# Block 0's gate and output projection taken out of the last stage and into the last round of the recurrence

## The reference, cut to what matters

```python
o = rwkv7_op(r, w, k2, v, -kk, kk * a)              # the recurrence over time, 2 sequences of 1024
o = o * gn_scale + gn_offset
o = o + rwkv                                        # the "bonus" term
x = x + (o * g) @ W_o                               # gate, then output projection, then residual
# then layer norm of x, a two-way switch, and expert 0 (gelu) or expert 1 (relu) per token
```

## Time and profile before

| what | us |
|---|---|
| median of 3 runs (1360.82, 1362.17, 1364.11) | 1362.17 |
| the profiled execution's own time | 1361.62 |
| its span, first to last instruction | 1359.6 |
| TensorE busy | 1229.7 (90%) |
| VectorE busy | 862.5 (63%) |
| ScalarE busy | 571.0 (42%) |
| GpSimd busy | 248.2 (18%) |
| last two hops of the recurrence begin | 1196.5 |
| last stage's first instruction | 1201.43 |
| last instruction's end (span) | 1359.6 |

### The profile page before, as it was taken

One profiled execution on the slowest core, in us unless ns is written; L12 is line 12 of the kernel. 1 busy time (PEld: TensorE's weight loads), 2 busy tenths in 40 slices (PEclk: granted clock), 3 DMA queues, 4 the chain that ended last, 5 costly groups with the idle time before them and its releaser, 6 DMA issues. The chain is left out here.

```text
span 1359.6 us, 32622 instructions
## 1 busy us (share of the span) xinstructions
PE 1229.7 (90%) x13048; PEld 714.2 (53%) x13080; DVE 862.5 (63%) x1742; ACT 571.0 (42%) x854; POOL 248.2 (18%) x444
## 2 busy tenths in 40 slices
PE   5769999999999999878999968995999999969998
PEld 2433333333333333254677644442888888857775
DVE  6367878888888888345433364897576666643432
ACT  2314777777777776823133214652211111112221
POOL 4220010000001001040277500233222111000000
PEclk9867999999999999998999988997999999979999
DMA  4310112211111220051143320000200000000000
GB/s 127 54 23 4 29 28 40 41 28 27 28 27 29 40 39 3 3 160 62 32 162 101 119 79 0 0 0 5 76 4 4 4 4 3 4 2 0 16 16 31
DMA packets 33836, 49.47 MB, mean 36 GB/s; under 512 B 11995, under 2 KB 22331, under 8 KB 32955
## 3 DMA queue, kind: packets, MB, share of 16 engines
q1 hardware_dynamic: 29211, 36.55, 12.1%
q0 software_dynamic: 3744, 10.23, 2.4%
q10 hardware_dynamic: 768, 1.05, 0.2%
HBM read 23.63 MB, written 9.31 MB: 24 GB/s over the span
## 5 line engine op out<-in xcount | busy, mean ns | idle before, releaser
L664 DVE TENSOR_REDUCE at_block_max<-at_p_ring 128x4 f32<-128x512 f32 x576 | 367.7, 686 | 76.3 <-PE at_p_ring L570 42.2
L641 ACT ACTIVATE at_probs<-at_p_score,abias 128x1024 f32<-128x1024 f32 (+2 forms) x320 | 318.8, 1029 | 123.2 <-PE at_p_score L600 69.0
L570 PE MATMUL at_p_ring<-kt,qt 64*128 64x128 bf16 (+3 forms) x1152 | 187.2, 284 | 18.5 <-PEq L727 7.4
L615 PE MATMUL at_p_out<-at_probs,at_vs 128*32 128x512 f32 (+3 forms) x1536 | 164.5, 500 | 0.4 <-ACT at_probs L641 0.4
L594 PE MATMUL at_p_score<-qt,kt 64*128 64x512 bf16 (+3 forms) x768 | 146.2, 332 | 5.7 <-ACT at_probs L641 4.8
L570 PEld LDWEIGHTS at_p_ring<-kt,qt 64*128 64x128 bf16 x1152 | 69.9, 95 | 130.4 <-DVE at_block_max L664 86.6
L707 POOL TENSOR_TENSOR at_shift<-shift,at_row_max 128x16 f32<-128x16 f32 x32 | 7.1, 221 | 423.2 <-DVE at_row_max L670 423.2
L594 PEld LDWEIGHTS at_p_score<-qt,kt 64*128 64x128 bf16 x768 | 38.4, 94 | 85.7 <-ACT at_probs L641 55.2
L2055 ACT COPY rc_ta<-rc_bank 128x256 f32<-128x256 f32 x32 | 10.3, 375 | 148.9 <-PE rc_bank L1826 148.9
L2184 PE MATMUL fi_p_in<-fi_xt,w_in 128*128 128x512 f32 x128 | 64.2, 626 | 0.7 <-ACT fi_xt L2221 0.7
L600 PE MATMUL at_p_score<-anticausal,ident 128*128 128x128 bf16 (+1 forms) x384 | 62.3, 244 | 0.0
(11 more groups left out here) (334 smaller groups left out, 2153.9 us busy)
## 6 DMA issues: line engine op xcount, KB each, us to landing
qt<-qparts SPq DMA_DIRECT2D x96, 64.0 KB, 2.4
kt<-kparts SPq DMA_DIRECT2D x96, 64.0 KB, 2.5
rows<-moe_chosen SPq DMA_DIRECT2D x4, 1024.0 KB, 4.8
w_routed<-in_w_routed_dram SPq DMA_DIRECT2D x1, 2816.0 KB
x<-in_x_dram SPq DMA_DIRECT2D x4, 512.0 KB, 8.4
moe_table<-rows SPq DMA_DIRECT2D x4, 512.0 KB, 2.7
out_dram<-x SPq DMA_DIRECT2D x4, 512.0 KB, 2.9
w_down<-in_w_down_dram SPq DMA_DIRECT2D x1, 1408.0 KB
```

What stands on the lines that cost most here:

```text
L570: mm = pe.matmul(bank[:, col:col + nb * P], qt[nxt][h * ROWS:(h + 1) * ROWS, pair, t * P:(t + 1) * P], kt[nxt][h * ROWS:(h + 1) * ROWS, pa ...
L615: mm = pe.matmul(p_out[32 * h:32 * h + 32, left(k):QC], vs[(now - e[2]) % BUFS][:, key, h, :], probs[g % PROBS][:, h % 2, at:at + w], star ...
L641: act.activation(probs[g % PROBS][:, :, 0:len(pairs) * w], p_score[g % 2][:, :, 0:len(pairs) * w], ACT.Exp, bias=abias[:, c * TPB + key:c ...
L664: dve.tensor_reduce(dst, src, AX.X, ALU.max).then_inc(s["fill_used"], 1)
```

## The change

GpSimd computes block 0's gate behind its last `y1`. TensorE computes block 0's projection at the end of the recurrence's last pass, behind the last hop, into banks 2 and 3 of `bank[0]`. VectorE adds it to x as the last thing in the recurrence's block. In the last stage gate(0) and project(0) are gone, add_projection(0) keeps only the statistics, and gate(1) stands behind normalise(0). The tile `gated0` is allocated outside both phases, and the recurrence phase also gets `vec`, `w_out` and `x`.

```diff
+        first_tiles = TB // P                       # 4
@@ TensorE, recurrence
+                def project_first(t, b):
+                    if last(t) and b == 0:
+                        pe.wait_ge(first_gated, EH)
+                        pe.wait_ge(loaded, len(pairs) * 16)
+                        pe.wait_ge(act_did[0], t * ACT_MARKS["each"])
+                        for tile in range(first_tiles):
+                            for h in range(EH):
+                                mm = pe.matmul(bank[0][:, 2 + tile // 2, tile % 2 * E:(tile % 2 + 1) * E],
+                                               gated[:, h, tile * P:(tile + 1) * P], w[:, h, :],
+                                               start=h == 0 and tile % 2 == 0, stop=h == EH - 1, skip_group_check=True)
+                        mm.then_inc(first_out, 1)
+
+                stages.append(project_first)
+                rounds(stages, (ys0, hop0, ys1, hop1, project_first))(pe)
@@ VectorE, recurrence, behind the last advance
+                dve.wait_ge(first_out, 1)
+                dve.tensor_tensor(x[:, 0:first_tiles, :], bank[0][:, 2:4, :].rearrange("p b (t e) -> p (b t) e", e=E),
+                                  x[:, 0:first_tiles, :], ALU.add)
@@ GpSimd, recurrence, behind the last y1
+                pool.wait_ge(y_out[0], first_tiles)
+                for h in range(EH):
+                    pool.tensor_scalar(gated[:, h, :], yt[:, h, 0, :], vec[:, h, VEC["gn_scale"]:VEC["gn_scale"] + 1], None,
+                                       ALU.mult).then_inc(first_scaled, 1)
+                pool.wait_ge(first_scaled, EH)
+                pool.tensor_tensor(gated[:, :, :], gated[:, :, :], data["bonus"][:, :, 0, :], ALU.add).then_inc(first_scaled, 1)
+                pool.wait_ge(first_scaled, EH + 1)
+                for h in range(EH):
+                    pool.tensor_scalar(gated[:, h, :], gated[:, h, :], vec[:, h, VEC["gn_offset"]:VEC["gn_offset"] + 1], None,
+                                       ALU.add).then_inc(first_scaled, 1)
+                pool.wait_ge(first_scaled, 2 * EH + 1)
+                for h in range(EH):
+                    pool.tensor_tensor(gated[:, h, :], gated[:, h, :], data["gt"][:, h, 0, :], ALU.mult).then_inc(first_gated, 1)
@@ last stage
-        gated = [sb(f"gated{i}", [P, EH, TB]) for i in range(2)]
+        gated = [gated0, sb("gated1", [P, EH, TB])]
@@ TensorE
                 def project(n):
-                    pe.wait_ge(gated_ready, (n + 1) * EH)
-                    if n:
-                        pe.wait_ge(tok_read, n)
+                    pe.wait_ge(gated_ready, n * EH)
+                    pe.wait_ge(tok_read, n)
...
-                project(0)
                 turn(0)
@@ VectorE
                 def add_projection(n):
-                    dve.wait_ge(proj_ready, n + 1)
...
-                    c.link(dve.tensor_tensor(tiles, p_work[:, :, :].rearrange("p b (t e) -> p (b t) e", e=E), tiles, ALU.add))
+                    if n:
+                        dve.wait_ge(proj_ready, n)
+                        c.link(dve.tensor_tensor(tiles, p_work[:, :, :].rearrange("p b (t e) -> p (b t) e", e=E), tiles, ALU.add))
...
-                gate(0)
-                gate(1)
                 add_projection(0)
                 normalise(0)
+                gate(1)
```

More of the change, by code:

```diff
@@ L1705, with recurrence_phase @@
 HOP_DONE = marks_of("s0a", "s0", "s1a", "s1")
-def recurrence_phase(nc, data, ident, masks, level_masks, level1_t, eye, yt, loaded, pairs):
+def recurrence_phase(nc, data, ident, masks, level_masks, level1_t, eye, yt, loaded, pairs, vec, w, x, gated):
     with ExitStack() as ctx:
@@ L1728, in recurrence_phase @@
         hop_made, hop_done, y_out = sem("hop_made"), sem("hop_done"), sem("y_out")
+        first_scaled, first_gated, first_out = (
+            ctx.enter_context(nc.semaphore("rc_" + n)) for n in ("first_scaled", "first_gated", "first_out"))
+        first_tiles = TB // P
         def flat(t):
@@ L1941, in _ @@
                 stages += [ta_, r_, yv, gh_(0), gh_(1)]
-                rounds(stages, (ys0, hop0, ys1, hop1))(pe)
+                def project_first(t, b):
[11 more added lines that the diff above has]
+                rounds(stages, (ys0, hop0, ys1, hop1, project_first))(pe)
             @block.vector
@@ L2112, with finish_phase @@
 TIE = 2.0 ** -25
-def finish_phase(nc, data, vec, w, x, stats, eps, ident, w_switch, w_in, b_in, w_back, b_back, out):
+def finish_phase(nc, data, vec, w, x, stats, eps, ident, w_switch, w_in, b_in, w_back, b_back, gated0, out):
     with ExitStack() as ctx:
@@ L2434, in two_blocks_program @@
         w_out = sb("w_out", [P, EH, E])
+        gated0 = sb("gated0", [P, EH, TB])
         ffn_pairs = [
@@ L2438, in two_blocks_program @@
             (w_back[:, :, :], halves(d["ffn_back"])), (b_back[:, :, :], d["ffn_b_back"])]
-        recurrence_phase(nc, data, ident, chunk_masks, level_masks, level1_t, eye, data["yt"], ffn_loaded, ffn_pairs)
-        finish_phase(nc, data, vec, w_out, x, stats, eps, ident, w_switch, w_in, b_in, w_back, b_back, out)
+        recurrence_phase(nc, data, ident, chunk_masks, level_masks, level1_t, eye, data["yt"], ffn_loaded, ffn_pairs, vec, w_out, x, gated0)
+        finish_phase(nc, data, vec, w_out, x, stats, eps, ident, w_switch, w_in, b_in, w_back, b_back, gated0, out)
 def shape_constants():
```

## The result

| | before | after |
|---|---|---|
| median, us | 1361.49 (6 runs, 1359.58 to 1364.11) | 1353.87 (6 runs, 1352.35 to 1361.70) |
| ratio | | 0.995, 95% interval 0.9927 to 0.9974 |
| the same kernel again, in a second session | 1360.42 (19 runs) | 1354.04 (5 runs), ratio 0.9945, 0.9932 to 0.9958 |

What follows compares the result with a forecast made beforehand. Bound by block 0's serial gate, projection, add and statistics, with TensorE's clock lowered by idling; 2.92 (gate) + 2.84 (clock) + 1.34 (tail), less 0.02, saves 7.08 us: 1362.17 to 1355.1, range 1352.2 to 1358.7.

Steps and rivals of the forecast that it cites:

- The sum: Last hop to block 0's add, plus boundary: 10.89 us before, 3.81 after, so 7.08 us saved.
- The split: Parts of the seam's saving: gate off path 2.92 us, projection at full clock 2.84, VectorE's tail beside projection 1.34.
- Gate on GpSimd at no cost: Block 0's gate: seven GpSimd instructions, 8.3 us (6.4 to 11.0), ending some 16 us before wanted; path cost 0.
- VectorE undisturbed: In round 7, GpSimd's gate slows VectorE by 0, at most 0.1 us; L1987 stays 425 ns.
- Projection at full clock: Block 0's 16 matmuls directly behind the last hop run at clock 1.00, taking 3.45 us instead of 6.29.
- Clock back at the same place in the work: Behind block 0's turn TensorE stays at 0.50 for 14.5 us as before, so this changes nothing.
- clock rival: Behind the turn, clock back late: saving 3.5 to 6 us, chance 0.19; early: 8.2 to 10.4 us, chance 0.11.
- What the trace of the changed kernel would show: Gate 1172.6 to before 1185, L1987 425 ns, projection 3.45 us, add near 1203.3, turn near 1208.4, full clock near 1223.

Runs made afterwards that it cites:

- Gate-only: Against the kernel before, only block 0's gate moves to GpSimd and gate(1) behind normalise(0); projection and add stay in the last stage: 1355.08 us, ratio 0.995.
- projection-only: Against the kernel before, block 0's projection and residual add move into the recurrence's block, its gate stays on VectorE, gate(1) behind normalise(0): 1360.60 us, ratio 1.0002.
- the changed kernel again: The changed kernel with no edit, run once more for a second trace: 1354.04 us.
- real work as the filler: Changed kernel with block 2 gated on GpSimd and its projection put on TensorE ahead of turn(0): 1343.98 us, ratio 0.9877 to before.

## Why the prediction was right, step by step

- *The sum.* 7.08 us forecast; from hop's end to the end of the span 7.10 in the first trace and 7.35 in the second. The medians give 7.6 and 6.4. The agreement to 0.02 is luck: at the turn the first trace has 6.93, and another 0.17 lies behind the turn, where I had forecast nothing. The forecast time also stands on a median of three runs, 1362.17; that of six is 1361.49.
- *The split.* Gate-only has 5.3 (forecast by the same terms 5.7), projection-only 0. The two moves are not two gains that add: the projection's place pays only once the gate is there in time. I had given parts (2.92, 2.84, 1.34) without saying this.
- *Gate on GpSimd at no cost.* The conclusion held, the size did not. I took 0.8 us for a tensor_scalar of 128x512 from the copy's row and bounded it at 1.37; it takes 1.57 to 1.61, so 11.5 in place of 8.3 us. The cover of 27 us made it harmless. The Trainium skill ("GPSIMD Engine Reference", section "4.1 Engine selection") says that GpSimd's one-input operations run roughly at line rate; this trace differs, the per-partition-scalar form costing more per column (1611 ns for 512) than the two-input tensor_tensor (1268 ns), and the measurement decides.
- *VectorE undisturbed.* Held: 425 ns beside the gate, and the same with three times the GpSimd work. The Trainium skill's rule on one SBUF input ("SBUF — State Buffer", section "Who interferes with whom") agrees, with GpSimd busy for 97% of the stretch where it was 31% in rows 7.
- *Projection at full clock.* Held, but 3.45 us was a size too small by 0.2. It is the share of block 1's projection in the chain of rows 1, counted from the end of the matmuls before; the same 16 take 3.62 us from their own start in that trace, and 3.72 here, of which 0.07 lies beside the hop. The add came 3.69 us behind the hop, forecast 3.49.
- *Clock back at the same place in the work.* Held: about 14 us behind the turn in both traces, 14.5 before. Neither clock rival came true. The reason that I gave, that the clock falls within the idle stretch, is so in the first trace only; in the second it fell as the turn began, which changed little. The larger sum was there, though: these 14 us cost 6 us, nearly as much as the whole change brings, and I treated them as given.
- *What the trace of the changed kernel would show* held in every point but the length of the gate.

## What to carry to other kernels

Before moving work off a serial passage, ask what the idle engine does to the clock of what follows: at this seam the idle 5 us of TensorE cost another 6 behind them. Look for work that is ready early (here another block's projection) and put it in the hole, rather than only shortening it. An engine with no later work, as GpSimd here, may do a thing four times slower for nothing, so long as its end is known to come before the first waiter.

## What I had not expected of the hardware

A single unexplained stop of TensorE of 3.1 us in one execution, and the half clock behind it, cost that execution 6 to 7 us, about as much as the change gains; a single trace's span would have shown "no change". The granted clock fell after 1.65 us of idleness in one trace (gate-only), held through 5.1 us in another (the changed kernel again), and held over 1.57 us in a third (real work as the filler).
